# Null-key attention of an eight-stage kernel: keys of six head pairs projected four stages earlier and kept in DRAM

## What is computed

```python
x = x + _L1_xattn_ref(_layernorm(x, axis=-1), ctx_2048, ...)   # third stage
...
# seventh stage, 16 heads of 64
q = _split_heads(jnp.einsum('bnd,df->bnf', x, Wq))
kv = jnp.einsum('bmc,cf->bmf', context, Wkv)
k, v = jnp.split(kv, 2, axis=-1)
k = jnp.concatenate((nk, k), axis=-2)
v = jnp.concatenate((nv, v), axis=-2)
attn = jax.nn.softmax(jnp.einsum('bhid,bhjd->bhij', q * scale, k), axis=-1)
out = jnp.einsum('bhij,bhjd->bhid', attn, v)
```

## Time and profile before

| | |
|---|---|
| runs of the kernel | 1116.24, 1118.69, 1119.89 us; median 1118.69 us |
| profiled execution, its own time | 1116.3 us |
| its span in the trace | 1114.5 us |
| busy: PE matmul, PE weight load, DVE, ACT, POOL | 88%, 65%, 74%, 57%, 38% |
| mean granted PE clock | 0.936 of full |
| front of the unmasked attention (first projection to end of the first passes) | 300.2 to 332.4 us |
| loop of the null-key attention | 876.6 to 1036.6 us |

### The profile page before, as it was taken

How to read it: one execution, slowest core, us unless ns; L and a number is a source line. 1 busy time by engine, 2 the same in 40 slices (tenths; PEclk the granted TensorE clock), 3 DMA queues, 4 the chain that set the end, 5 groups by cost and what they waited for, 6 DMA issues and landing times.

```text
span 1114.5 us, 18229 instructions
## 1 busy us (share of the span) xinstructions
PE 979.7 (88%) x5958; PEld 720.5 (65%) x5958; DVE 823.2 (74%) x1980; ACT 636.2 (57%) x1594; POOL 426.2 (38%) x664
## 2 busy tenths in 40 slices
PE   5688999999759998868999999996899999998587
PEld 4457887888513434746777777775667777777465
DVE  7855898898667881698989988768665667675663
ACT  3373666766317775366797877973144666664121
POOL 8231122111121110235766767767130565654200
PEclk9697999999859998899999999997899999999789
DMA  5530211122052310300000000303000100003000
GB/s 215 139 122 1 76 39 39 39 67 62 20 170 81 98 40 20 152 1 1 1 1 1 1 1 1 151 1 121 1 1 21 57 1 2 1 14 138 1 1 20
DMA packets 32254, 53.55 MB, mean 48 GB/s; under 512 B 4192, under 2 KB 24448, under 8 KB 31008
## 3 DMA queue, kind: packets, MB, share of 16 engines
q1 hardware_dynamic: 29616, 50.03, 13.5%
q10 hardware_dynamic: 2544, 2.36, 0.7%
HBM read 45.33 MB, written 6.88 MB: 47 GB/s over the span
## 4 chain that ended last, share of the span: by engine, by line
PE 64%; DVE 16%; ACT 9%; issue 6%; DMA 2%; POOL 1%; SPq 1%; DVEq 0%; ACTq 0%
PE psum L1733 8%; PE psum L1356 8%; PE psum L1366 7%; ACT region_d L1795 4%; PE psum L2524 3%; PE psum L1763 3%; PE psum L2453 3%; PE psum L412 3%; PE psum L368 2%; DVE region_d L1931 2%; ACT region_c L1812 2%; PE psum L1719 2%; PE psum L2427 2%; PE psum L2469 2%; DVE null_work L2626 2%
## 5 line engine op out<-in xcount | busy, mean ns | idle before, releaser
L1733 PE MATMUL psum<-gated_parts 128*128 128x512 f32 x768 | 191.1, 400 | 18.7 <-DVE region_d L1931 15.1
L1733 PEld LDWEIGHTS psum<-gated_parts 128*128 128x128 f32 x768 | 137.0, 188 | 69.1 <-DVE region_d L1931 36.8
L2024 POOL TENSOR_TENSOR region_d<-region_d 128x256 f32<-128x256 f32 x126 | 94.6, 751 | 93.1 <-DVE region_d L1931 91.0
L1425 ACT ACTIVATE rounds_work<-psum,region_c 128x512 f32<-128x512 f32 x128 | 84.6, 688 | 28.1 <-PE psum L1356 25.9
L802 DVE TENSOR_REDUCE work<-psum 128x1 f32<-128x512 f32 x128 | 81.8, 686 | 22.0 <-PE psum L368 20.3
L1356 PE MATMUL psum<-parts,split 128*128 128x512 f32 x384 | 95.9, 400 | 0.0
L1366 PE MATMUL psum<-parts,split 128*128 128x512 f32 x384 | 93.3, 392 | 0.0
L1547 POOL CAST parts<-rounds_work 128x1024 fp32r<-128x1024 f32 x32 | 33.4, 1043 | 151.9 <-ACT rounds_work L1425 151.9
L1795 ACT ACTIVATE region_d<-psum,gated_work 128x128 f32<-128x128 f32 x256 | 75.9, 447 | 26.8 <-issue 22.2
L1479 DVE TENSOR_TENSOR parts<-rounds_work,parts 128x1024 fp32r<-128x1024 f32 x64 | 76.3, 1220 | 16.9 <-POOL parts L1547 15.9
L1795 ACT ACTIVATE region_d<-psum,ctx 128x128 f32<-128x128 f32 x256 | 73.0, 375 | 25.2 <-PE psum L1733 15.4
(11 more groups left out here) (450 smaller groups left out, 2190.6 us busy)
## 6 DMA issues: line engine op xcount, KB each, us to landing
rounds_work<-cw_rows SPq DMA_DIRECT2D x32, 256.0 KB, 3.4
region_a<-in_l1v SPq DMA_DIRECT2D x8, 512.0 KB, 4.0
region_b_last<-in_l1o SPq DMA_DIRECT2D x1, 4096.0 KB, 12.3
region_a<-in_l2f SPq DMA_DIRECT2D x1, 4096.0 KB, 12.0
region_b_last<-in_l3f_small SPq DMA_DIRECT2D x1, 4096.0 KB, 12.8
region_a<-in_l3f SPq DMA_DIRECT2D x1, 2080.0 KB, 7.4
region_c<-in_l0f SPq DMA_DIRECT2D x1, 2076.0 KB, 12.3
region_c<-in_l3x SPq DMA_DIRECT2D x1, 2048.0 KB, 7.8
```

Of the source, the lines that this page charges most:

```text
L1425: act.activation(H[g % 2][:, f, :], bank[f], ACT.Gelu_apprx_tanh, bias=W("b1")[:, (g % E) * FT + f:(g % E) * FT + f + 1]).then_inc(h_ready ...
L1733: ins = pe.matmul(bank[2 * (n % 2) + c], src[a][:, t * P:(t + 1) * P], weights[b][:, piece(c)], start=m == 0, stop=m == len(PASSES) - 1)
L2024: pool.tensor_tensor(tile[:, 0:2, :], tile[:, 0:2, :], tile[:, 2:4, :], ALU.add).then_inc(k.pool_chain, 1)
```

## The change

Three things change.

1. **In the unmasked attention**, PE also projects the keys of pairs 2 to 7 of the null-key attention (12 halves of 512 tokens), as plain float32 products, each half in four quarters: 128x256 columns, two terms. 24 quarters stand between its own projections and the first first pass; the other 24 stand one behind each first pass of the 12 first steps. They go to PSUM banks 4 to 7. ACT copies the 12 halves to SBUF: 3 behind its last split, 3 between the stores of the second half's query parts, 6 at every second step. The first second pass waits for all 12 copies. SP stores them to a DRAM tensor `null_keys` (256 KB each, two after each of the weight pieces 1 to 6 that it loads there). The weights come by one DMA of 1 MB which SP issues at the start of the second stage.
2. **In the null-key attention**, PE no longer projects those halves, and POOL no longer splits their weights. SP loads each half back from DRAM to SBUF, into the place of the split key weights, one pair ahead. ACT and DVE still make the high and low part of each, with the SBUF copy as their source.
3. **The plan of the steps** becomes, from pair 1 on: step 0 query half 0 and key half 0; step 1 value chunk 0 and key half 1; step 2 query half 1; step 3 value chunk 1.

The core of the diff:

```diff
+class NullKeysAhead:
+    PAIRS = range(2, 8)
+    BANKS = (4, 5, 6, 7, 4, 5, 6, 4, 5, 6, 4, 5)
+    def load_weights(self, sp):
+        sp.dma_start(self.weights, self.k.dram["l3x"][:, 0:2048].rearrange("p (c n) -> p c n", c=2))\
+            .then_inc(self.loaded.semaphore, 16)
+    def quarter(self, pe, j):
+        n, q, c = j // 4, j % 4 // 2, j % 2
+        if j % 4 == 0 and self.BANKS[n] in self.BANKS[:n]:
+            last = max(m for m in range(n) if self.BANKS[m] == self.BANKS[n])
+            pe.wait_ge(*self.copied.at(last + 1))
+        ins = pe.matmul(k.bank[self.BANKS[n]][:, q * HALF // 2:(q + 1) * HALF // 2], self.weights[:, c, pair * P:(pair + 1) * P],
+                        k.ctxT[:, c, first:first + HALF // 2], start=c == 0, stop=c == 1)
+    def copy(self, act, n):
+        act.wait_ge(*self.psum.at(n + 1))
+        act.activation(self.keys[n], self.k.bank[self.BANKS[n]], ACT.Copy).then_inc(self.copied.semaphore, 1)
+    def store(self, sp, n):
+        sp.wait_ge(*self.copied.at(n + 1))
+        sp.dma_start(self.k.dram["null_keys"][n * P:(n + 1) * P, :], self.keys[n]).then_inc(self.stored.semaphore, 16)
...
 packed_attention, PE
+            for j in range(AHEAD):
+                keys.quarter(pe, j)
             pe.wait_ge(*rest.at(first_of(3)))
...
                 first_pass(b, PER * u)
+            if not masked and i < LAG:
+                keys.quarter(pe, AHEAD + 2 * i)
...
+                if not masked and s == 0:
+                    pe.wait_ge(*keys.copied.at(keys.HALVES))
                 second_pass(*divmod(s, STEPS))
...
                 first_pass(b, PER * u + 1)
+            if not masked and i < LAG:
+                keys.quarter(pe, AHEAD + 2 * i + 1)
...
 packed_attention, SP
                 k.load_piece(sp, "l1v", v, UNITS * B)
+                for n in range(2 * v - 2, 2 * v):
+                    if 0 <= n < keys.HALVES:
+                        keys.store(sp, n)
...
 null_key_attention
-        for b, chunks in enumerate(((("q", 0), ("k", 0)), (("q", 1), ("k", 1)), (("v", 0),), (("v", 1),))):
+        plan = ((("q", 0), ("k", 0)), (("q", 1), ("k", 1)), (("v", 0),), (("v", 1),))
+        if p >= 1:
+            plan = ((("q", 0), ("k", 0)), (("v", 0), ("k", 1)), (("q", 1),), (("v", 1),))
+        for b, chunks in enumerate(plan):
...
+    HERE = [n for n, (what, p, h) in enumerate(MADE) if what != "k" or p < keys.PAIRS[0]]
+    k32 = [null_w[:, 4 * T + 20 * P + h * HALF:4 * T + 20 * P + (h + 1) * HALF].bitcast(F32) for h in range(2)]
...
                 for n in MADE_IN[p][b]:
-                    project(n)
+                    if n in HERE:
+                        project(n)
...
 ACT
-            src = bank_of(n)
-            act.wait_ge(proj_psum, n + 1)
+            if loaded(what, p):
+                src = k32[h]
+                act.wait_ge(*keys_loaded[h].at(16 * (p - keys.PAIRS[0] + 1)))
+            else:
+                src = bank_of(n)
+                act.wait_ge(proj_psum, HERE.index(n) + 1)
...
 DVE
-            src = bank_of(n)
+            src = k32[h] if loaded(what, p) else bank_of(n)
             dve.wait_ge(proj_sb, n + 1)
...
 SP
+        for p in keys.PAIRS:
+            for h in range(2):
+                if p == keys.PAIRS[0]:
+                    sp.wait_ge(proj_psum, projected("k", p - 1, 1))
+                else:
+                    sp.wait_ge(*proj_low.at(LOWS[MADE.index(("k", p - 1, h))]))
+                n = 2 * (p - keys.PAIRS[0]) + h
+                sp.dma_start(k32[h], k.dram["null_keys"][n * P:(n + 1) * P, :]).then_inc(keys_loaded[h].semaphore, 16)
```

More of the change, by code:

```diff
@@ L214, in packed_attention @@
     RX = [k.carve(F32, NH * SLOT) for _ in range(2)]
-    if masked:
+    if not masked:
+        keys.place([k.carve(F32, HALF) for _ in range(4)])
+    else:
         k.carve_from(WORK - 5 * T // 2)
@@ L510, in scalar @@
             parts, cols = piece(2 * pair + 1)[2:]
+            if not masked and pair == 1:
+                for n in range(3):
+                    keys.copy(act, n)
             for i in range(3):
@@ L517, in scalar @@
                     store(act, q_dram, NH, parts[i], row, cols).then_inc(stored_q[pair].semaphore, 16)
+                if not masked and pair == 1:
+                    keys.copy(act, 3 + i)
         def context_part(n):
@@ L548, in scalar @@
             s = i - LAG
+            if not masked and i < LAG and i % 2 == 1:
+                keys.copy(act, (AHEAD + 2 * i + 2) // 4 - 1)
             if not masked and i % SU == 0 and 0 < i <= ALL:
@@ L1553, in sync @@
     def sync(sp):
+        sp.wait_ge(k.x_tiles, NT * number)
+        keys.load_weights(sp)
         for s in range(TURNS):
@@ L2405, in null_key_attention @@
     cleared = k.count("experts_cwT_sb", 2)
+    keys_loaded = [k.count(f"packed_{what}_psum", 8 * keys.HALVES) for what in ("k", "q")]
     def tensor(pe):
```

81 lines of the change are left out of this document (60 added, 21 removed).

## The result

The changed kernel is slower. Its median is 1125.84 us (20 runs, 1117.05 to 1136.80) against 1118.53 us for the kernel before in the same job (20 runs, 1115.23 to 1121.08). The ratio is 1.0046, 95% interval 1.0026 to 1.0066, that is 2.9 to 7.4 us more with 5.1 us as the middle. (The ratio leaves out the five of the changed kernel's executions that took over 1.5% more than its fastest one, the profiled one among them, so it is smaller than the quotient of the medians.) The forecast was 1.7 us less. Not only the middle moved: the runs of the changed kernel spread over 20 us, those before over 6 (8 to 16 in the later jobs of this study). The profiled execution took 1133.87 us (span 1132.0), and 11.6 us of its distance to the profile before lie in the first stage, whose code is the same; the first two experiments deal with that, and I compare stage by stage.

A forecast was written before the change was run, and what follows sets the result against it. Null-key steps 0 and 1 were taken as PE-bound, steps 2 and 3 as a DVE-PE circle with a 4.65 us floor. Gains of 1.0 (loop) and 0.7 (front) make 1.7: 1118.7 to 1117.0 us, range 1112.0 to 1121.0.

The forecast's parts named there:

- The step that failed: Front of the unmasked attention: 12 steps of two first passes and two quarters, 1.43 us each against 1.39, 0.5 lost.
- The quarter's price: Front, PE: a new 128x256 plain float32 matmul at full clock takes 0.46 us, between 0.43 and 0.49.
- the start: Front: with 24 quarters ahead, the first passes start 0 to 0.9 us late, taken as 0.4.
- The rival in which weight loads don't overlap: Front: quarters take 0.8 us each, 9 us late and 9 us more in the steps; chance 0.02.
- DVE as the bound of the steps: Front: the 12 steps before take 1.39 us each, with DVE busy 14.88 of 16.90 us.
- The clock: Front: PE's clock stays at its upper level instead of 0.50; value projections gain 0.3 us, first second-pass steps 1.3.
- Null-key loop: Steps 0 and 1 leave PE's bound; DVE's key low part waits for POOL; 1.0 us gained, 0.4 to 1.7.
- an order that the prediction had left open: Null-key step 1, pairs 1 to 5: DVE's low part or POOL's cast first; 0.14 us gained or 0.10 lost.
- Stores, loads, the 1 MB of weights: SP's 12 stores, the loads of the key halves and the weights' DMA are hidden and cost nothing.

The follow-up runs named there:

- the first two experiments: First: the changed kernel again, unedited (1131.94 us), and three variants of it; second: the kernel before again, unedited, one run, 1119.91 us.
- e1: The changed kernel again, unedited, for a second profiled execution: median 1131.94 us, ratio 1.0121 to the kernel before.
- e14: e4 with the null-key order of e13, nothing left out: 1117.19 us, ratio 0.9990 to the kernel before.
- e15: e7 with the null-key order of e13 for its four pairs: 1120.90 us, ratio 1.0012 to the kernel before.
- e6: The changed kernel with only pairs 5 to 7 projected early, 24 quarters, all ahead of the first passes: 1121.46 us, ratio 0.9988 to the kernel before.
- after: The first profiled execution of the changed kernel, unedited: 1133.87 us.
- e2: The changed kernel with quarters and their loads kept, but every key projected in the null-key loop by the old plan: 1126.87 us, ratio 1.0090.
- e4: The changed kernel with both quarters of a step behind its second first pass: 1121.20 us, ratio 1.0030 to the kernel before.
- e10: e4 with the null-key order of e9, nothing left out: 1120.35 us, ratio 1.0022 to the kernel before.
- e9: e3 with the null-key plan reordered: at most one low part in a step, the key ahead of the values: 1115.75 us, ratio 0.9971.
- e13: e9 with ACT's copy of a loaded key one step earlier, its low part on DVE in the step with values: 1112.37 us, ratio 0.9946.
- e3: The changed kernel without quarters and ACT's copies; SP stores pieces of the context in place of the keys: 1117.75 us, ratio 1.0005.
- e7: The changed kernel with only pairs 4 to 7 projected early, 24 quarters ahead and one in each of 8 steps: 1123.25 us, ratio 1.0024.
- e8: e3 with the old plan of steps in the null-key loop: 1118.92 us, ratio 1.0000 to the kernel before.

## Why the prediction was wrong

- **The step that failed** is "each of the 12 steps then holds two first passes ... and two quarters: 1.32 to 1.54 us ... I take 1.43". It measured 1.90. The sum took each kind of matmul at the pace it has among its own: 2 x (0.43 + 0.23) = 1.32, its lower bound. Between the two kinds the quarter takes 0.20 more and the first pass 0.09 more, twice a step: 1.90. The bounds held no price for the change itself. It was not an unknown: the trace of before has it further on, at full clock, where a first pass (L368) stands ahead of the float32 weighted values (L412) and behind them:
```profile
353.84 0.38 PE L368 MATMUL psum<-work 48*128 48x512 bf16 x1
354.15 0.64 PE L412 MATMUL psum<-work 128*32 128x256 f32 x8
354.72 0.39 PE L368 MATMUL psum<-work 48*128 48x512 bf16 x1
```
  The first pass takes 0.31 there, not 0.23, and the next first pass starts 0.31 us behind the last of the eight L412 records, where the kinds in a row have 0.22 to 0.24. 12 x (1.90 - 1.43) = 5.6 us, most of the 6.8 between the 1.7 forecast as gained and the 5.1 lost by the ratio.
- **The quarter's price** was right: 0.43 in a row, 0.447 with the wait, forecast 0.46 (0.43 to 0.49). So was **the start**: in seven of the profiles with quarters the first pass starts 4.1 to 4.3 us behind DVE's last split, against 3.9 to 4.3 in the seven without; in the other three (e1, e14, e15) it starts at 4.4 to 5.0, and waited for a DMA. The rival in which weight loads don't overlap (0.8 us a quarter) is false for quarters in a row; one alone, at 0.63, lies halfway.
- **DVE as the bound of the steps** was misread. 14.88 us busy of 16.90 looked like a bound; DVE's pace in a row is 0.60, and the steps were 1.39 by the handshake with first passes at half clock (e6).
- **The clock** went as forecast in the front, 1.00, and in five of the ten profiles with quarters the gain behind it is there: "next" 14.12 to 15.61 for 15.76 (after, e2, e4, e10, e14). In the other five it is 16.6 to 19.9, with slow stretches. "Rest" is 88.8 and 88.7 us in after and e2 where the profiles without quarters have 86.0 to 87.5; the others have 85.9 to 88.1, e6 94.3. The prediction took the stretch that it looked at and let the rest of the stage stand. How much the clock costs on average is not shown: these are single executions, and the times don't settle it, since the kernel before spreads over up to 16 us in later jobs and e14, with quarters, over 8.
- **Null-key loop**: right in mechanism, a little better in size. 4.88 and 4.87 for 4.90 and "4.90 to 5.14"; 1.7 us for 1.0, the upper end of its range, because in step 1 DVE came ahead of POOL's cast, an order that the prediction had left open. The Trainium skill, page SBUF — State Buffer, section "Who interferes with whom", has the loser of the two blocked for the other's whole length; e9 and e13 agree with it from both sides, 1.46 us for DVE when it starts second, 0.59 instead of 0.19 for POOL when POOL does.
- **Stores, loads, the 1 MB of weights** at nothing: right as far as is shown. e3 has all of these transfers, its stages are those of before but for the loop's 1.7 us, and its ratio is 1.0005 [0.9983, 1.0028].

Together the profiles give 5.7 us in the steps and 0.8 to 1.3 behind them (e2 and after, against a mean of 102.3 without quarters; 4.7 in e1), less 1.7 in the loop: 4.8 to 5.3 us, which is the ratio's 5.1. So much is accounted for in the first job. In the second the account falls short: e1's ratio says 9.3 to 17.7 us where its stages have 8.7, and e4's 1.0 to 5.7 where they have none. Why the same program had medians of 1125.8 and 1131.9 us in two jobs stays open. Between the first stage and the first of these maxima the 17 profiles take 234.0 to 236.3 us, between this stage and the loop 443.9 to 446.8, behind the loop 92.4 to 95.1; the first stage, with 79.9 to 91.5, is where executions differ most outside the stage of the change.

## What to carry to other kernels

Filling an idle engine is not free where the filler alternates with the work that is there: put the new matmuls in one run (the 24 ahead cost nothing), or one to a step that has room for it (e7: 1.36 us, no longer than before), and look in the old trace for a row in which one kind follows the other: the price of the change can stand there. Where one engine's instruction with two SBUF inputs meets POOL's, ask which of them is released first: moving its input's copy a step ahead brought 2.8 us in the loop against e9 and 2.0 against e8, more than the 1.7 that removing 16.7 us of PE work had brought. And before explaining a difference in a stage that was not touched, profile the old kernel twice.

## What was not expected of the hardware

- A 128x256 float32 matmul on the whole array between first passes on 48 rows: 0.63 us instead of 0.43, and 1.06 instead of 0.86 for two. The weight load behind each change starts 0.23 to 0.33 us late with nothing shown to wait for. Why was not tried: the two kinds differ in data type and in the part of the array that they use. The trace of before has the same 0.31 us between first passes and float32 matmuls on 128 rows and 32 columns (353.84, 354.15), so the whole array isn't needed for it.
- Two first passes side by side in 0.32 us, as long as one (e4, 330.36), where both were ready.
- The slow stretch of the clock in the front sat at the same place in all seven profiles without quarters, and not there in the ten with them; the same untouched first stage took 79.9 to 91.5 us.
